# A last batch's routing moved among attention tiles, a square root behind one scatter, another output bank, and earlier norms, in a gated cross-attention and mixture-of-experts block

## The chip, the cores and the metric

The kernel runs on one core of one Trainium2 chip. The metric is the device time of one execution in microseconds; lower is better.

## The reference

Sixteen batches of 112 tokens with 512 channels pass through a gated cross-attention and then a gated mixture of experts. Everything is fp32.

```
x = x + tanh(g_xattn) * xattn(layernorm(x), ctx)      # ctx: 16 x 375 x 128, 16 heads, rotated queries and keys
x = x + tanh(g_ffn)   * ffn(layernorm(x))
ffn: logits = x @ gate_w.T                            # 64 experts
     topv, topi = top_k(logits, 8); rw = softmax(topv)
     out = sum over the 8 chosen e of rw_e * down_e(silu(gate_e(x)) * up_e(x))
     out = out + sigmoid(x @ sh_gate1.T) * shared_expert(x)
```

## The kernel before

**Stages.** The attention goes through four groups g = 0 to 3 of four batches. A group has a head loop (h = 0 to 17) and then an attention loop (t = 0 to 62). In the head loop TensorE does for each head a projection (12 matmuls of 448 columns, `project`), the latent product (9 matmuls, `latent`), and, two heads behind, the product with the folded key weights (`to_context`); VectorE multiplies by cosines and sines (seven operations for a head, the rotation, in `latent`), and GpSimd adds the two parts. In the attention loop each step t takes one tile of 128 rows of scores: `score_tile`, a softmax over four engines, `turn_tile` (transposes, four steps later) and `attend` (once in four tiles). `out_head` then projects a batch's 16 heads to the 512 output channels; batches 12, 13 and 14 have theirs at step HALF = 49 of the last group, batch 15 (`LAST`) from step 57 on, two heads at 57, two at 59, twelve behind the loop.

**Routing of one batch.** It is cut into steps which every engine issues at the same place of its own written-out order (`finish(step, b)`): *stats* (VectorE takes mean and variance, GpSimd the power -1/2 in `spread`), *norm* (VectorE; SyncE then stores the rows and the base), *turn* (4 transposes on TensorE, a copy on ScalarE), *router* (8 short matmuls), *choose* (VectorE: top 8, mask, weights; 2.4 us), *rank* (two pairs of matmuls that count earlier tokens of each expert), *place* (VectorE: the row number of each of the 8 copies), *scatter 0* to *7* (GpSimd: eight indirect DMAs that put the token's row into the expert's slots in DRAM, `slot_rows`). VectorE counts its results of a batch in `s_route`, 16 for each; the wait of a step for 15 or 16 of a batch is a wait for *place*. Batches are strictly in order, since *rank* uses the running `count`.

**Where the steps stand.** Batches 0 to 11 are routed one group later in the head loop by `slots` and `between` (slots 2h and 2h + 1), or, the last ones of a group, beside the output heads (`held`, `beside`). A group's first routed batch has stats in slot 0, norm in slot 2 and turn in slot 3; slot 2 comes, on VectorE, behind the rotation of head 0. Batch 12 is routed in steps HALF + 1 to HALF + 11 of the last attention loop (`LATE`). Batches 13 and 14 are `held(NG)`: turn, router and rank stand beside batch 15's heads 4, 5, 9 (batch 13) and 7, 10, 15 (batch 14). Behind them GpSimd issues batch 13's eight scatters, the power for batch 15, and batch 14's eight scatters. `END` then routes batch 15 and orders the experts by load (*order*), with its own eight scatters last.

**Banks.** Batch 15's output stands in PSUM bank 7, which batch 12's routing also uses, so head 0 waits for batch 12's *place* (L993). Banks 0 to 2 hold scores.

**Experts.** `load_expert` reads an expert's weights (768 KB), `load_slots` its token rows (up to 612 KB) once all scatters have landed (`wait_attention_over`). For each expert TensorE transposes the rows (`turn`), multiplies by gate and up (`inner`) and by the down weights (`down`); VectorE and ScalarE split each operand in a high and a low part. SyncE issues expert 0's weights when the order is known, then slots 0, weights 1, slots 1, weights 2, slots 2 to 4. The results are scattered to `parts`, from which the last stage sums.

```python
                if p == NG and h == 0:
                    pe.wait_ge(s_exp, RT * B)
                    pe.wait_ge(s_route, NR * (B - GB + 1))
...
            sp.wait_ge(s_order, 1)
            load_expert(0)
            wait_attention_over(sp)
            for x in range(NXE):
                load_slots(sp, x)
                if 1 <= x + 1 < NE:
                    load_expert(x + 1)
```

Of the kernel before, what the change touches and what calls it, by code (L numbers as in the profile page):

```python
# [29 lines left out]
GB = 4  # L30
# [81 lines left out]
NR = 16  # L112
# [23 lines left out]
def slots(g, i):  # L136

    at = START[LEFT[g]][i]
    whole = {"turn": at + 3, "router": at + 4, "choose": at + 5, "rank": at + 7, "place": at + 8}
# [19 lines left out]
def held(p):  # L159

    if p == NG:
        return [B - 3, B - 2]
# [11 lines left out]
LATE_LOADED = 16 * 13  # L174
FIRST_LATE = B - GB
LATE = {HALF + 1: ("norm", FIRST_LATE), HALF + 2: ("turn", FIRST_LATE), HALF + 3: ("norm", FIRST_LATE + 1),
        HALF + 4: ("router", FIRST_LATE), HALF + 5: ("choose", FIRST_LATE), HALF + 6: ("norm", FIRST_LATE + 2),
        HALF + 7: ("rank", FIRST_LATE), HALF + 8: ("place", FIRST_LATE), HALF + 9: ("scatter low", FIRST_LATE),
        HALF + 11: ("scatter high", FIRST_LATE)}

# [26 lines left out]
def route_banks(b):  # L207
# [5 lines left out]
    if b in held(NG):  # L213
        return 0, 1 + b % 2, 3
# [5 lines left out]
def out_bank(b):  # L220
    return OUT_BANK[b % GB] if b < B - GB else 4 + b % GB
# [61 lines left out]
def build(nc, a, out):  # L283
    with ExitStack() as ctx:
# [252 lines left out]
        def sync(sp):  # L537
# [166 lines left out]
            for g in range(NG):  # L704
# [40 lines left out]
                for t in range(GB * RT + ALL_LAGS):  # L745
# [5 lines left out]
                    if g == NG - 1 and LATE.get(t):  # L751
                        finish(*LATE.get(t))
# [66 lines left out]
        def tensor(pe):  # L819
# [157 lines left out]
            def out_head(p, h, part):  # L977
# [82 lines left out]
            for g in range(NG):  # L1060
# [21 lines left out]
                for t in range(GB * RT + ALL_LAGS):  # L1082
# [5 lines left out]
                    if g == NG - 1 and LATE.get(t):  # L1088
                        finish(*LATE.get(t))
# [60 lines left out]
            for x in range(E + 1):  # L1150
# [4 lines left out]
                if x >= 1:  # L1155
                    down(x - 1)
# [57 lines left out]
        def vector(dve):  # L1214
# [217 lines left out]
            for g in range(NG):  # L1432
# [24 lines left out]
                for t in range(GB * RT + ALL_LAGS):  # L1457
# [10 lines left out]
                    if g == NG - 1 and LATE.get(t):  # L1468
                        finish(*LATE.get(t))
# [93 lines left out]
            turn(0)  # L1563
            find_own(0)
# [6 lines left out]
            for x in range(E + 1):  # L1571
# [518 lines left out]
```

## Time and profile before

| | |
|---|---|
| median of 3 runs | 1543.54 us (1543.45 to 1543.58) |
| the profiled execution | 1545.0 us, its span 1543.1 us |
| TensorE busy | 1419.2 us (92%) |
| VectorE, GpSimd, ScalarE busy | 1147.3, 783.3, 672.1 us |
| mean granted TensorE clock | 0.970 of full speed |
| DMA | 380.10 MB, mean 246 GB/s |

The span runs from the first to the last instruction on the profiled core. The program's four attention groups take its first two thirds (to about 1070 us), the experts run from about 1104 to 1451 us, and the rest is the final sum.

### The profile page before, as it was taken

What the parts mean: (1) busy time and instruction counts of PE and PEld (TensorE: products, weight loads), DVE (VectorE), ACT (ScalarE), POOL (GpSimd) and SP (SyncE); (2) the same over time, 40 slices, a digit from 0 to 9 for tenths busy, and PEclk for the clock granted to TensorE, in tenths of its full rate; (3) what the DMA queues carried; (4) which work ended last, traced back from release to release, by engine and by line L of the source; (5) the groups of instructions that cost most, each with busy time, mean ns of one, the idle gap of its engine ahead of it and who ended that gap; (6) DMA issues with size and microseconds to landing.
All of it is one profiled execution on the core that took longest, in us unless ns stands there. A gap on an engine that the chain in (4) does not pass through costs nothing.

```text
span 1543.1 us, 25067 instructions
## 1 busy us (share of the span) xinstructions
PE 1419.2 (92%) x7674; PEld 1165.1 (76%) x7674; DVE 1147.3 (74%) x2601; ACT 672.1 (44%) x1558; POOL 783.3 (51%) x858
## 2 busy tenths in 40 slices
PE   6999899899999989999989999986399999989985
PEld 5767787777788777778877778864388999979742
DVE  5777783298987269989528988544488999979587
ACT  3332673011476011177301137431277777867521
POOL 4555673145775458877345786325344344334322
PEclk9999999999999999999999999998599999999998
DMA  7898896355697757830365763295899999999698
GB/s 238 298 313 314 274 286 193 112 167 188 215 307 219 265 162 246 253 122 8 104 217 191 243 216 113 86 341 180 239 331 327 332 357 366 373 339 338 206 429 344
DMA packets 164359, 380.10 MB, mean 246 GB/s; under 512 B 20200, under 2 KB 55682, under 8 KB 162434
## 3 DMA queue, kind: packets, MB, share of 16 engines
q1 hardware_dynamic: 136182, 286.33, 55.5%
q0 software_dynamic: 20608, 62.28, 11.8%
q10 hardware_dynamic: 7436, 29.88, 6.0%
q8 instruction: 64, 1.05, 0.3%
q14 instruction: 69, 0.57, 0.1%
HBM read 238.82 MB, written 139.59 MB: 245 GB/s over the span
## 4 chain that ended last, share of the span: by engine, by line
PE 71%; DVE 10%; DMA 9%; issue 5%; POOL 2%; ACT 2%; SPq 1%; POOLq 0%; another core or an unknown queue 0%; DVEq 0%; ACTq 0%
PE bank L822 18%; PE bank L824 17%; PE bank L823 17%; PE bank L926 8%; PE bank L955 4%; DMA p_in<-parts 3%; PE bank L1124 2%; DMA parts<-y_sb,to_row 1%; DMA w_ex<-in_w_ex 1%; PE bank L914 1%; PE bank L904 1%; DMA out<-p_sum 1%; DVE prob_t0l L1309 1%; POOL slot_rows L1962 1%; ACT prob L1705 1%
## 5 line engine op out<-in xcount | busy, mean ns | idle before, releaser
L1940 POOL TENSOR_TENSOR q_rope<-q_rope,q_sin 128x448 f32<-128x448 f32 x192 | 215.7, 1153 | 147.4 <-DVE q_sin L1274 146.8
L2020 POOL DMA_INDIRECT parts<-y_sb,to_row x140 | 138.3, 988 | 221.0 <-ACT y_sb L1846 191.4
L1946 POOL TENSOR_TENSOR prob<-prob,row_inv 128x375 f32<-128x375 f32 x219 | 176.8, 814 | 88.7 <-DVE row_inv L1296 86.5
L1962 POOL DMA_INDIRECT slot_rows<-rows,pos_i x112 | 109.7, 980 | 104.2 <-DVE count L1384 76.8
L1274 DVE TENSOR_TENSOR q_sin<-bank,sin_q 128x448 f32<-128x448 f32 (+1 forms) x256 | 158.5, 619 | 4.0
L926 PE MATMUL bank<-q_rope,m_w 128*128 128x448 f32 x384 | 155.7, 541 | 2.8 <-issue 1.8
L1288 DVE TENSOR_REDUCE row_max<-bank 128x1 f32<-128x375 f32 x224 | 118.9, 535 | 36.8 <-PE bank L824 36.4
L1705 ACT ACTIVATE prob<-bank,row_max 128x375 f32<-128x375 f32 x224 | 128.3, 573 | 9.1 <-DVE row_max L1288 9.1
L1846 ACT ACTIVATE y_sb<-bank,own 96x512 f32<-96x512 f32 (+4 forms) x140 | 90.9, 687 | 68.6 <-PE bank L824 62.0
L955 PE MATMUL bank<-ident,prob 128*125 128x128 f32 x672 | 113.6, 279 | 7.1 <-DVE prob_t0l L1309 3.6
L1270 DVE TENSOR_TENSOR q_rope<-bank,cos_q 128x448 f32<-128x448 f32 x192 | 118.3, 616 | 0.0
L955 PEld LDWEIGHTS bank<-ident,prob 128*125 128x125 f32 x672 | 103.6, 189 | 15.9 <-POOL prob L1946 13.1
L926 PEld LDWEIGHTS bank<-q_rope,m_w 128*128 128x128 f32 x384 | 71.5, 189 | 53.4 <-issue 50.3
L1688 ACT ACTIVATE q_th<-bank 128x448 fp32r<-128x448 f32 x64 | 34.9, 545 | 170.6 <-PE bank L926 156.4
L1681 ACT ACTIVATE q_hk0h<-bank 128x448 fp32r<-128x448 f32 x32 | 17.5, 546 | 160.4 <-PE bank L824 160.4
L1720 ACT ACTIVATE prob_t0h<-bank 125x384 fp32r<-125x384 f32 x128 | 63.0, 492 | 46.0 <-PE bank L955 46.0
L1124 PE MATMUL bank<-ident,x_g 96*128 96x96 f32 (+4 forms) x560 | 64.5, 261 | 20.0 <-DMA x_g<-slot_rows 20.0
L1124 PEld LDWEIGHTS bank<-ident,x_g 96*128 96x128 f32 (+4 forms) x560 | 59.5, 144 | 29.6 <-DMA x_g<-slot_rows 20.5
L822 PE MATMUL bank<-xg_t0h,w_gu_s0h 128*128 128x224 f32 (+5 forms) x256 | 75.9, 297 | 4.9 <-DVE e_half L1529 4.9
L1342 DVE SCALAR_TENSOR_TENSOR x_sb<-bank,tanh_g,x_sb 112x512 f32<-112x512 f32 x16 | 11.3, 746 | 88.5 <-PE bank L824 88.5
L822 PE MATMUL bank<-xg_t1h,w_gu_s1h 128*128 128x224 f32 (+5 forms) x256 | 73.9, 289 | 0.7 <-DVE e_half L1529 0.6
L823 PE MATMUL bank<-xg_t0l,w_gu_s0h 128*128 128x224 f32 (+5 forms) x256 | 73.2, 286 | 0.0
(364 smaller groups left out, 4399.1 us busy)
## 6 DMA issues: line engine op xcount, KB each, us to landing
w_ex<-in_w_ex SPq DMA_DIRECT2D x64, 768.0 KB
slot_rows<-blank SPq DMA_DIRECT2D x64, 612.0 KB
p_in<-parts SPq DMA_DIRECT2D x14, 2048.0 KB, 16.9
m_w<-m_dram SPq DMA_DIRECT2D x48, 192.0 KB
x_g<-slot_rows ACTq DMA_DIRECT2D x16, 476.0 KB
wq_s0h<-wq_dram SPq DMA_DIRECT2D x24, 256.0 KB
wq_s0l<-wq_dram SPq DMA_DIRECT2D x24, 256.0 KB
wq_s1h<-wq_dram SPq DMA_DIRECT2D x24, 256.0 KB
```

What stands on the lines that cost most here:

```text
L822: pe.matmul(out_ap, wh, mh, start=first, stop=False)
L823: pe.matmul(out_ap, wh, ml, start=False, stop=False)
L824: return pe.matmul(out_ap, wl, mh, start=False, stop=last)
L926: m = pe.matmul(bank[5][:, 0:GT], m_w[n % NW][:, c, :], q_rope[h % 2][:, c, :], start=(c == 0), stop=(c == QC - 1))
L955: m = pe.transpose(bank[bk][0:LP, j * P:(j + 1) * P], prob[n % NP][:, j * LP:(j + 1) * LP], ident[:])
L1124: m = pe.transpose(bank[n % 3][:, j * size:(j + 1) * size], x_g[x % NXE][0:size, t, j * P:(j + 1) * P], ident[0:size, 0:size])
L1274: dve.tensor_tensor(q_sin[to:to + size, other, :].rearrange("p (b s) -> p b s", b=GB), src[at:at + size], table, ALU.mult).then_inc(s_rope, 1)
L1705: act.activation(prob[i][:], bank[score_bank(n)][:, 0:L], ACT.Exp, bias=row_max[:, i:i + 1], accum_out=row_sum[:, i:i + 1]).then_inc(s_exp, 1)
L1940: pool.tensor_tensor(o[:, c, :], o[:, c, :], q_sin[:, c, :], ALU.add).then_inc(s_radd, 1)
L1946: pool.tensor_tensor(prob[i][:], prob[i][:], row_inv[:, i:i + 1].to_broadcast([P, L]), ALU.mult)\
L1962: pool.indirect_dma_start(slot_rows, bass.IndirectOffsetOnAxis(ap=pos_i[i][:, k:k + 1], axis=0), rows[i][:], None).then_inc(s_slots[i], 16)
L2020: pool.indirect_dma_start(parts, bass.IndirectOffsetOnAxis(ap=to_row[x % NROW][0:size, t:t + 1], axis=0), y_sb[x % NY][t][0:size, :], None)\
```

## The change

It has five parts. (1) The first routed batch of a group has its norm in slot 1 and its turn in slot 2, so the norm is issued on VectorE ahead of head 0's rotation. (2) Batch 13's turn, router, choose, rank, place and all eight scatters stand in steps HALF + 9 to HALF + 12 of the last attention loop; only batch 14 is held, at heads 4, 5 and 9. (3) Batch 15's output stands in bank 2; head 0 waits no longer for batch 12's place, and batch 13's turn waits until batch 12's ranks have been read from bank 7. (4) GpSimd takes batch 15's power behind scatter 0 of batch 14. (5) The weights of experts 0 to 2 are all issued when the order is known; expert 0's `inner` is issued before expert 1's `turn`, on VectorE and ScalarE too, with both splits of weights ahead; slots 5 are loaded behind `inner(0)` as before.

```diff
-    whole = {"turn": at + 3, "router": at + 4, ...
+    whole = {"turn": at + (3 if i else 2), "router": at + 4, ...
-    return {"stats": max(0, at - 2), "norm": max(2, at), **(whole if i < GB - LEFT[g] else {})}
+    return {"stats": max(0, at - 2), "norm": at if i else 1, **(whole if i < GB - LEFT[g] else {})}
...
-        return [B - 3, B - 2]
+        return [B - 2]
...
-          NG: ({"turn": 4, "router": 5, "rank": 9}, {"turn": 7, "router": 10, "rank": 15})}.get(
+          NG: ({"turn": 4, "router": 5, "rank": 9},)}.get(
...
+STATS_AT = 1
-        HALF + 7: ("rank", FIRST_LATE), HALF + 8: ("place", FIRST_LATE), HALF + 9: ("scatter low", FIRST_LATE),
-        HALF + 11: ("scatter high", FIRST_LATE)}
+        HALF + 7: [("rank", FIRST_LATE)], HALF + 8: [("place", FIRST_LATE)],
+        HALF + 9: [("scatter low", FIRST_LATE), ("turn", FIRST_LATE + 1)], HALF + 10: [("router", FIRST_LATE + 1)],
+        HALF + 11: [("scatter high", FIRST_LATE), ("choose", FIRST_LATE + 1)],
+        HALF + 12: [("rank", FIRST_LATE + 1), ("place", FIRST_LATE + 1), ("scatter low", FIRST_LATE + 1),
+                    ("scatter high", FIRST_LATE + 1)]}
...
-        return 0, 1 + b % 2, 3
+        return 0, 1, 3
...
 def out_bank(b):
+    if b == LAST:
+        return 2
...
-                    pe.wait_ge(s_route, NR * (B - GB + 1))
...
+                    elif b == B - GB + 1:
+                        pe.wait_ge(s_route, NR * (b - 1) + R_RANKED)
...
-            load_expert(0)
+            for x in range(NE):
+                load_expert(x)
             wait_attention_over(sp)
             for x in range(NXE):
                 load_slots(sp, x)
-                if 1 <= x + 1 < NE:
-                    load_expert(x + 1)
...
             turn(0)
-            for x in range(E + 1):
+            inner(0)
+            turn(1)
+            for x in range(1, E + 1):
...
-                    if b == LAST - 1:
-                        finish("stats", LAST)
-                    finish("scatter low", b)
-                    finish("scatter high", b)
+                    for k in range(TOP):
+                        if b == LAST - 1 and k == STATS_AT:
+                            finish("stats", LAST)
+                        finish(f"scatter {k}", b)
```

## Rows read from the trace of the kernel before

**Rows 1.** The page: the chain that ended last, share by engine

```profile
PE 71%; DVE 10%; DMA 9%; issue 5%; POOL 2%; ACT 2%; SPq 1%; POOLq 0%; another core or an unknown queue 0%; DVEq 0%; ACTq 0%
```

**Rows 2.** Windows: stretch, then busy us per engine, granted clock, DMA share, GB/s

```profile
1064.00:1110.00 46.00, 12.90 (x61) 10.21 (x60) 17.92 (x69) 4.38 (x10) 23.98 (x26) 0.58 0.70 216
1300.00:1400.00 100.00, 95.18 (x731) 87.48 (x729) 89.71 (x213) 74.35 (x135) 36.91 (x39) 0.97 1.01 351
```

**Rows 3.** Timeline, TensorE at the starts of groups 1, 2, 3: start, duration, instruction, idle before

```profile
303.65 1.01 PE L1028 MATMUL bank<-ident,early_rows 112*128 112x112 f32 x4 [4.17 <-DVE early_rows L1399]
...
308.10 0.37 PE L822 MATMUL bank<-q_hk1h,wcq_s1h 128*128 128x448 f32 x1
...
548.19 0.37 PE L822 MATMUL bank<-q_hk0h,wcq_s0h 128*128 128x448 f32 x1
...
549.82 0.36 PE L824 MATMUL bank<-q_hk0h,wcq_s0l 128*128 128x448 f32 x1
554.35 1.01 PE L1028 MATMUL bank<-ident,rows 112*128 112x112 f32 x4 [4.17 <-DVE rows L1399]
...
559.65 0.36 PE L822 MATMUL bank<-q_hk1h,wcq_s1h 128*128 128x448 f32 x1
...
806.42 1.01 PE L1028 MATMUL bank<-ident,rows 112*128 112x112 f32 x4 [4.17 <-DVE rows L1399]
```

**Rows 4.** Timeline, GpSimd and VectorE at the start of group 2

```profile
548.38 0.57 POOL L1906 TENSOR_TENSOR ln_stats<-ln_stats,minus_half 112x1 f32<-112x1 f32 x1
...
549.50 0.61 DVE L1270 TENSOR_TENSOR q_rope<-bank,cos_q 128x448 f32<-128x448 f32 x1
...
553.58 0.71 DVE L1399 TENSOR_SCALAR rows<-x_sb,ln_stats 112x512 f32<-112x512 f32 x1
```

**Rows 5.** Timeline, the last attention steps and batch 15's heads

```profile
1040.91 0.24 ACT L1705 ACTIVATION_READ_ACCUMULATOR prob<-bank,row_max 128x1 f32 x1
...
1043.98 0.55 DVE L1309 TENSOR_TENSOR prob_t0l<-bank,prob_t0h 125x384 fp32r<-125x384 f32 x1
...
1044.32 0.74 PE L822 MATMUL bank<-v_w0h,q_th 128*112 128x512 f32 x1 [3.23 <-DVE count L1384]
...
1047.92 0.48 PE L822 MATMUL bank<-prob_t0h,kv_r1h 125*128 125x512 f32 x1
...
1068.03 0.40 PE L824 MATMUL bank<-v_w2h,q_tl 128*112 128x512 f32 x1
```

**Rows 6.** Timeline, VectorE on batch 15: residual, norm, slot numbers

```profile
1069.64 0.74 DVE L1342 SCALAR_TENSOR_TENSOR x_sb<-bank,tanh_g,x_sb 112x512 f32<-112x512 f32 x1
...
1075.69 0.55 DVE L1399 TENSOR_SCALAR rows<-x_sb,ln_stats 112x512 f32<-112x512 f32 x1 [4.36 <-POOL ln_stats L1904]
...
1083.78 0.17 DVE L1383 CAST pos_i<-place 112x8 int32<-112x8 f32 x1
```

**Rows 7.** Timeline, GpSimd: first scatter of batch 12 and of batch 13

```profile
1044.23 1.06 POOL L1962 DMA_INDIRECT slot_rows<-rows,pos_i  x1 [1.76 <-DVE count L1384]
...
1064.53 0.94 POOL L1962 DMA_INDIRECT slot_rows<-rows,pos_i  x1 [10.51 <-DVE count L1384]
```

**Rows 8.** Timeline, SyncE's issues and TensorE at the experts' start

```profile
1089.99 0.01 SPq L774 DMA_DIRECT2D w_ex<-in_w_ex  x1
1099.21 0.34 SPq L533 DMA_DIRECT2D x_g<-slot_rows  x1
...
1103.91 2.18 PE L1124 MATMUL bank<-ident,x_g 96*128 96x96 f32 x12 [16.61 <-DMA x_g<-slot_rows]
...
1111.37 0.59 PE L822 MATMUL bank<-xg_t0h,w_gu_s0h 128*128 128x288 f32 x1
...
1117.64 0.38 PE L822 MATMUL bank<-xg_t1h,w_gu_s1h 128*128 128x288 f32 x1
```

**Rows 9.** The chain in order of time: start, us, what

```profile
1094.57 3.19 DMA slot_rows<-rows,pos_i
...
1361.91 16.17 DMA w_ex<-in_w_ex
```

More of the change, by code:

```diff
@@ L138, in slots @@
     at = START[LEFT[g]][i]
-    whole = {"turn": at + 3, "router": at + 4, "choose": at + 5, "rank": at + 7, "place": at + 8}
+    whole = {"turn": at + (3 if i else 2), "router": at + 4, "choose": at + 5, "rank": at + 7, "place": at + 8}
     if g:
         whole.update({f"scatter {k}": at + 9 + (k * 7 // 8 if i == 2 else k) for k in range(TOP)})
-    return {"stats": max(0, at - 2), "norm": max(2, at), **(whole if i < GB - LEFT[g] else {})}
+    return {"stats": max(0, at - 2), "norm": at if i else 1, **(whole if i < GB - LEFT[g] else {})}
 def between(g, slot):
@@ L174 @@
 LATE_LOADED = 16 * 13
+STATS_AT = 1
 FIRST_LATE = B - GB
[L176 to L179 removed]
+LATE = {HALF + 1: [("norm", FIRST_LATE)], HALF + 2: [("turn", FIRST_LATE)], HALF + 3: [("norm", FIRST_LATE + 1)],
+        HALF + 4: [("router", FIRST_LATE)], HALF + 5: [("choose", FIRST_LATE)], HALF + 6: [("norm", FIRST_LATE + 2)],
+        HALF + 7: [("rank", FIRST_LATE)], HALF + 8: [("place", FIRST_LATE)],
[3 more added lines that the diff above has]
+                    ("scatter high", FIRST_LATE + 1)]}
 LAST = B - 1
@@ L750, in sync @@
                         load_early()
-                    if g == NG - 1 and LATE.get(t):
-                        finish(*LATE.get(t))
+                    for step, b in LATE.get(t, ()) if g == NG - 1 else ():
+                        finish(step, b)
                     if t < GB * RT:
@@ L1087, in tensor @@
                             out_head(NG - 1, h, "all")
-                    if g == NG - 1 and LATE.get(t):
-                        finish(*LATE.get(t))
+                    for step, b in LATE.get(t, ()) if g == NG - 1 else ():
+                        finish(step, b)
                     if 0 <= t - TURN_LAG < GB * RT:
@@ L1154, in tensor @@
                     inner(x)
-                if x >= 1:
-                    down(x - 1)
+                down(x - 1)
             def body(eng, r, x):
@@ L1467, in vector @@
                         project_out(NG - 1)
-                    if g == NG - 1 and LATE.get(t):
-                        finish(*LATE.get(t))
+                    for step, b in LATE.get(t, ()) if g == NG - 1 else ():
+                        finish(step, b)
                     if attend_at(t - 1):
@@ L1562, in vector @@
             split_expert(0)
-            turn(0)
-            find_own(0)
+            split_expert(1)
             dve.tensor_scalar(l_room, bank[7][0:1, E:2 * E], float(-TR), 0.0, ALU.add, ALU.max).then_inc(s_rounds, 1)
@@ L1570, in vector @@
             dve.tensor_tensor(starts[:], l_at, l_first, ALU.add).then_inc(s_rounds, 1)
-            for x in range(E + 1):
+            turn(0)
+            inner(0)
+            find_own(0)
+            turn(1)
+            find_own(1)
+            for x in range(1, E + 1):
                 if x + 1 < E:
@@ L1783, in scalar @@
                             finish("choose", b)
-                    if g == NG - 1 and LATE.get(t):
-                        finish(*LATE.get(t))
+                    for step, b in LATE.get(t, ()) if g == NG - 1 else ():
+                        finish(step, b)
                     if attend_at(t - 1):
@@ L1849, in scalar @@
             split_expert(0)
+            split_expert(1)
             turn(0)
-            for x in range(E + 1):
+            inner(0)
+            load_slots(act, NXE)
+            turn(1)
+            for x in range(1, E + 1):
                 if x + 1 < E:
@@ L1996, in gpsimd @@
                         project_out(NG - 1)
-                    if g == NG - 1 and LATE.get(t):
-                        finish(*LATE.get(t))
+                    for step, b in LATE.get(t, ()) if g == NG - 1 else ():
+                        finish(step, b)
                     if EARLY_SCORES <= t - 2 < GB * RT:
```

3 lines of the change are left out of this document (1 added, 2 removed).

## The prediction

> **What bounds the kernel now.** I read first the chain that ended last [rows 1]: 71% of it is TensorE, 10% VectorE, 9% DMA. TensorE is busy 92% of the span, so a change can gain only where it is left waiting, and what a wait is worth must be read at its place. I then went through the stretches in windows, and the low ones are two kinds. One is the stretch in which batch 15 is finished and the experts start, 1064 to 1110: TensorE is busy 12.9 of 46.0 us at a granted clock of 0.58, and GpSimd, with 24.0 us, is the busiest engine [rows 2]. The other is short: in the timelines of TensorE at the starts of groups 1, 2 and 3 there is the same hole of 4.17 us each time, in front of the four transposes (L1028) of the group's first routed batch, ended by VectorE's norm [rows 3]. The experts' stretch is different: from 1300 to 1400 TensorE is busy 95.2 of 100 us, VectorE 89.7, and the DMA share is 1.01 [rows 2]. There nothing is gained by order alone, but a later start or an earlier one is passed on to the end.
>
> **Part 1, the groups' first norm.** Group 2 shows why the hole is there [rows 3, 4]. TensorE issues its last matmul of head 0's latent product at 549.82 and would turn the routed batch next. GpSimd has that batch's power ready at 548.38 + 0.57 = 548.95. But VectorE begins the rotation at 549.50, and its norm stands behind it and begins at 553.58; the transposes start at 554.35. With the norm ahead, VectorE takes it at about 549.1 (0.15 behind the power, an estimate for the hand-over) and ends by 549.8, when TensorE comes. So the hole goes: 3 x 4.17 = 12.5 us.
>
> What it costs: VectorE waits some 1.1 us for GpSimd's power ahead of head 1's projection split, and the norm holds that split and the rotation up by about 0.6 us. Behind them queue GpSimd's additions and, a head later, `to_context`. The cover is TensorE's own work between: 12 matmuls of projection and 9 of the next latent product, 21 x 0.204 = 4.3 us (0.204 is the step from 548.19 to 549.82 over eight [rows 3]). The rotation takes 553.58 - 549.50 = 4.1 us, so it ends at about 554.2, GpSimd's last addition at about 555.8, and `to_context` of head 0 starts behind turn, projection, latent product and router at about 555.4 and asks for the last third a little after 556.5. It holds, with under 1 us to spare; if that cover were gone, each group would give back up to 0.6 us. SyncE stores rows and base one slot earlier, two issues of some 0.34 us each (as another load's [rows 8]), ahead of loads needed over 4 us later: nothing.
>
> The hole has a second price. Behind it the granted clock is at its lower level, 1.2 of 2.4 GHz: in group 2 turn and projection take 559.65 - 554.35 = 5.30 us. At the full level 12 x 448 + 4 x 112 columns at 0.204 us for 448 are 2.7 us. That is 2.6 us, in group 1 (308.10 - 303.65 = 4.45) 1.75 us, and for group 3 I take group 2's [rows 3]. Without a hole TensorE runs straight on, as it did up to 549.82. Sum 7.0 us; the bounds are 0 and 7.0 (a little work might still be slow), and I take 7.0, since the four transposes are then all that interrupts dense matmuls.
>
> Part 1: 19.5 us.
>
> **Parts 2 to 4, up to the last scatter.** Head 0 of batch 15 started at 1044.32 after 3.23 us for batch 12's place. What it still needs is the last exponential, 1040.91 + 0.24 = 1041.15 [rows 5]. So heads 0 and 1 start at 1041.3, 3.0 us earlier. Into the next two steps come batch 13's turn, its copy on ScalarE and its router. VectorE's low part of tile 53, which the transposes of tile 55 need, is still behind batch 12's place and ends at 1044.53 [rows 5]. `attend` of block 2 started at 1047.92; it can't start before about 1045.0 now, nor later than 1047.9 unless the copy stalls. I take 1046.2, since turn, copy and router are a round trip of some 2 us, part of it under other transposes. From there to the end of batch 15's heads were 1068.43 - 1047.92 = 20.5 us; batch 13's turn and router (about 1 us, from the 1.01 us of four transposes at the low clock [rows 3] and eight shorter matmuls) have left it: 19.5. The heads end at 1065.7 (1064.5 to 1067.4).
>
> GpSimd now. From 1064.53 to 1094.57 it starts 24 scatters and one power, so one each (30.04 - 1.15) / 23 = 1.25 us [rows 7, 9]. Batch 12's eight run from 1044.23 to 1054.2 as before. Batch 13's place needs rank, behind `attend` (9 matmuls) and heads 2 and 3: about 1050, and 2.4 us on VectorE: 1052.5, before GpSimd is free. So batch 13's scatters, which started at 1064.53, are done at 1064.2. Scatter 0 of batch 14 ends at 1065.5. Batch 14's turn, router and rank stand where batch 13's stood, 3 us earlier, so its place is ready by then.
>
> Residual and statistics of batch 15 took from 1069.64 to 1075.69 - 4.36 = 1071.33, 1.7 us; VectorE comes to them only when batch 14's place is done, 1.2 us late. Now it is free: 0.1 + 1.7, then addition and power, 1.1 with hand-overs (the power 0.57 [rows 4]). The norm starts 2.9 us behind the last head: 1068.6 against 1075.69 [rows 6]. GpSimd stands idle for 2 us in front of that power, which is harmless only as far as the following queue isn't the later end: fifteen scatters follow, the last starts at 1068.7 + 14 x 1.25 = 1086.2. Batch 15's place ends 8.3 us behind its norm (1083.95 - 1075.69 [rows 6]), 1076.9, and its first scatter is due at 1077.5, so GpSimd stays the bound, narrowly. Last scatter 1094.57 to 1086.2: 8.4 us.
>
> **Part 5.** The first weights were issued 14.3 us behind the norm (1089.99); now at 1082.9, and three of them, 2.36 MB. At 351 GB/s [rows 2] that is 6.7 us alone, but the scatters (112 rows of 2176 bytes in 1.25 us, 195 GB/s) run until 1087. I get 1092.5 for the third weight. The first slots' load was issued 4.6 us behind the last scatter's start, landed 4.7 us later [rows 8, 9], and is now issued at 1090.8, so it can stand behind weights for 1.6 us, or, if the scatters come first, up to 1.57 MB / 351 = 4.5 us; below nothing is excluded, since it was alone before. I take 1.0. The rows arrive at 1103.91 - 8.4 + 1.0 = 1096.5: 7.4 us gained (3.9 to 9.5).
>
> The Trainium skill (DMA: Bandwidth & Descriptors, Queues, rings and completion order) says that each DMA engine takes turns between its queues packet by packet. By that the scatters' packets would wait beside the weights' and the last one would land later than its 3.19 us; if it shared evenly, its 244 KB would take twice as long, about 0.7 us more by 351 GB/s. No row before shows scatters beside three weights.
>
> From the first rows' arrival to expert 1's `inner` were 1117.64 - 1103.91 = 13.7 us [rows 8]. Now: transposes and splits 3.4, `inner(0)` 5.5 (1111.37 on, low clock), `turn(1)` 1.6, its splits on ScalarE and VectorE 2 to 2.5, of which `turn(2)` hides its own time only: 13.0. That is 0.7 us (0 to 2), since the wait for expert 1's splits takes the place of the one for its rows.
>
> **Sum.** 12.5 + 7.0 + 7.4 + 0.7 = 27.6 us, off a span of 1543.1: 1515.5. The profiled execution took 1545.0, the median of the runs is 1543.54, 0.4 above that span: 1515.9.
>
> **Rivals.**
> 1. *The weights hold up the slots.* For it: one queue, in order, and 1.57 MB more ahead of the slots. Against: they are issued 8 us before. It costs up to 4.5 instead of 1.0: 1519.4. Chance 0.13.
> 2. *The experts catch up.* The chain has a weight load of 16.17 us at 1361.91 [rows 9], the only big wait in the experts' stretch, and TensorE lost 4.8 of 100 us there [rows 2]. With two weights out of the opening rush the DMA is 4.5 us ahead: up to that much more gained, 1511.4. Against: a load waits for its buffer, so a lead is not kept. Chance 0.12.
> 3. *The groups' wait returns one step later.* TensorE would wait for the copy, the delayed rotation or a weight load, each time, and keep part of the hole. If it keeps half of hole and clock, 9.7 us: 1525.6. For it: under 1 us to spare. Against: VectorE idles after the old norm. Chance 0.08.
> 4. *The DMA makes it slower.* The share is 1.01 from 1300 to 1400 [rows 2]. If the new order of loads made each of the 64 experts wait longer for weights, the gain is gone from 27.6 / 64 = 0.43 us an expert on; at 0.5 us it is 32.0: 1547.9. Against: the bytes are the same and SyncE's order from expert 3 on is too. Chance 0.02.
> 5. *Nothing moves*: parts 1 to 4 each take away a wait that TensorE or GpSimd shows in its own timeline, so 0.01.
>
> The forecast itself, 1512.5 to 1519, has 0.64. About 0.2% (3.1 us) is what a measurement can tell from no change. Faster 0.96, same 0.01, slower 0.03. Down to rival 2 and up beyond rival 1: 1510.5 to 1521.5.
>
> **What would show it.** In the timeline of TensorE no idle time in front of L1028 in groups 1 to 3, and 0.204 us steps behind it; VectorE's norm ahead of the first rotation. Head 0 at about 1041.3 - 19.5 = 1021.8; batch 13's scatters without a pause behind batch 12's; the norm of batch 15 at 1049, the last scatter's start at 1066.7, the first rows at 1077, all on the new time axis. The forecast is wrong if GpSimd's queue has a pause before batch 14's scatter 1 longer than 4 us, if the first slots take over 7 us to land, or if the experts' stretch, 347 us from 1104 to 1451, is not 346 to 347.

## The result, and the profile after

The changed kernel takes 1523.55 us (median of 4 runs, 1520.89 to 1530.97), the kernel before 1543.56 us in the same rounds (1543.45 to 1544.13): a ratio of 0.9877, 95% interval 0.9843 to 0.9912, so 20.0 us faster. The forecast was 1515.9 us with a range of 1510.5 to 1521.5. The direction is right; the gain is 7.6 us smaller than forecast, and the time lies above the range. The profiled execution took 1523.96 us for a span of 1522.1.

The chain that ended last (compare [rows 1]) is still TensorE's, with two points less of it and two more of GpSimd:

```profile
PE 69%; DMA 10%; DVE 10%; issue 5%; POOL 4%; ACT 2%; SPq 0%; POOLq 0%; ACTq 0%; DVEq 0%
```

Lines after have other numbers: L827 to L829 are the three products of a split matmul, L1034 the turn, L1046 the router, L1406 the norm, L1920 the power, L1976 the scatter, L1130 the transposes of an expert's rows. At the start of group 2 TensorE's timeline has no hole in front of the turn (it was 4.17 us, [rows 3]):

```profile
542.38 0.36 PE L827 MATMUL bank<-q_hk0h,wcq_s0h 128*128 128x448 f32 x1
...
542.79 0.37 PE L829 MATMUL bank<-q_hk0h,wcq_s0l 128*128 128x448 f32 x1
543.00 0.55 PE L1034 MATMUL bank<-ident,rows 112*128 112x112 f32 x4
...
543.81 0.36 PE L829 MATMUL bank<-xn_th,wq_s0l 128*128 128x448 f32 x1
544.01 0.36 PE L827 MATMUL bank<-xn_th,wq_s0h 128*128 128x448 f32 x1
```

The four transposes take 0.55 us instead of 1.01, the steps behind them are 0.2 us, and the granted clock is 1.00 there (0.50 behind the hole before). From the turn to the next latent product (`q_hk1h`) it takes 2.88, 2.84 and 2.83 us in groups 1, 2 and 3, where it took 4.45, 5.30 and 5.32, and none of the three has a hole. Late attention on TensorE, with batch 13's turn and router among the heads (compare [rows 5]):

```profile
1021.02 0.56 PE L960 MATMUL bank<-ident,prob 128*125 128x128 f32 x3 [1.08 <-DVE prob_t0l L1316]
1021.75 0.46 PE L827 MATMUL bank<-v_w0h,q_th 128*112 128x512 f32 x1 [0.16 <-DVE q_tl L1322]
...
1023.21 0.55 PE L1034 MATMUL bank<-ident,rows 112*128 112x112 f32 x4
...
1040.49 0.39 PE L829 MATMUL bank<-v_w2h,q_tl 128*112 128x512 f32 x1
```

VectorE's norm of batch 15 and GpSimd's first and last scatter of the last four batches (compare [rows 6, 7]):

```profile
1046.78 0.55 DVE L1406 TENSOR_SCALAR rows<-x_sb,ln_stats 112x512 f32<-112x512 f32 x1 [4.17 <-POOL ln_stats L1920]
```

```profile
1024.72 1.06 POOL L1976 DMA_INDIRECT slot_rows<-rows,pos_i  x1 [1.76 <-DVE count L1391]
1026.09 0.94 POOL L1976 DMA_INDIRECT slot_rows<-rows,pos_i  x1 [0.30 <-issue]
...
1064.39 0.94 POOL L1976 DMA_INDIRECT slot_rows<-rows,pos_i  x1 [0.30 <-issue]
```

The pause of 10.51 us in front of batch 13's first scatter [rows 7] is gone, 32 scatters (those of batches 12 to 15) run on end with one power among them, and the last one starts 30.2 us earlier than the 1094.57 of before. From there the lead shrinks. The chain in order of time (compare [rows 9]) has this scatter's landing at 8.66 us, where it was 3.19:

```profile
1064.39 8.66 DMA slot_rows<-rows,pos_i
1073.97 4.71 DMA x_g<-slot_rows
```

What the DMA moved in that landing, by queue (packets, MB, share of the 16 engines; q0 carries GpSimd's scatters, q1 SyncE's loads), before (1094.57 to 1097.76) and after (1064.39 to 1073.05):

```profile
q0 software_dynamic: 264, 0.77, 69.6%
q1 hardware_dynamic: 2, 0.01, 0.5%
```

```profile
q1 hardware_dynamic: 296, 1.60, 46.7%
q0 software_dynamic: 359, 1.05, 30.1%
```

The scatters alone are more than the last one's 244 KB: earlier ones are still on their way when it is issued. After, 1.60 MB of weights move beside them.

And the experts' start, in the timelines of SyncE, TensorE and ScalarE (compare [rows 8]; the last four are the load of slots 5 that ScalarE issues, ScalarE's split of expert 1's rows, the next expert's transposes, and expert 1's first product):

```profile
1059.72 3.37 SPq L780 DMA_DIRECT2D w_ex<-in_w_ex  x3
...
1073.97 5.07 SPq L539 DMA_DIRECT2D x_g<-slot_rows  x5
...
1078.72 2.18 PE L1130 MATMUL bank<-ident,x_g 96*128 96x96 f32 x12 [20.32 <-DMA x_g<-slot_rows]
...
1089.79 0.40 ACTq L539 DMA_DIRECT2D x_g<-slot_rows  x1
1090.23 1.25 ACT L1831 ACTIVATE xg_t1h<-bank 128x384 fp32r<-128x384 f32 x3 [4.40 <-DVE to_row L1566]
1091.46 2.15 PE L1130 MATMUL bank<-ident,x_g 96*128 96x96 f32 x12 [2.48 <-DVE xg_t1l L1520]
...
1093.32 0.59 PE L827 MATMUL bank<-xg_t1h,w_gu_s1h 128*128 128x288 f32 x1
```

The slots' load takes 4.8 us from issue to the transposes, as before. Expert 1's first product is 14.6 us behind the first rows, where it was 13.7, and ScalarE had stood idle for 4.40 us just before.

The windows from expert 1's first product to the last store of parts, before and after:

```profile
1117.64:1453.82 336.18, 329.81 (x2472) 300.32 (x2471) 301.52 (x699) 256.25 (x463) 137.34 (x140) 0.99 0.97 331
```

```profile
1093.32:1432.43 339.11, 332.28 (x2471) 301.90 (x2470) 301.13 (x697) 256.11 (x462) 136.23 (x139) 0.99 0.94 322
```

The stretch is 2.9 us longer. In its middle, from 1300 to 1400, TensorE is as busy as in [rows 2], and the DMA share is the same:

```profile
1300.00:1400.00 100.00, 95.22 (x734) 87.04 (x733) 90.04 (x213) 74.22 (x135) 37.42 (x38) 0.98 1.01 350
```

Laid end to end, the lead on the span is: 19.5 us at the last transposes in front of batch 15's head 0 (1040.53 to 1021.02), 30.2 at the last scatter, 25.2 at the first rows (1103.91 to 1078.72), 24.3 at expert 1's first product, 21.4 at the last store (1453.82 to 1432.43), 21.0 at the end (1543.1 to 1522.1). The forecast had 27.9, 26.9, 27.6 and 27.6 for the last scatter, the rows, expert 1 and the end.

### The profile page after: what moved, and what is told of

It is laid out like the page before. It is cut to its first block, busy times and chain, and to the rows that moved or that the text cites. A ratio compares the mean times of both kernels' runs of the same rounds, so it can differ in the third digit from the quotient of the medians.

```text
span 1522.1 us, 25067 instructions
## 1 busy us (share of the span) xinstructions
PE 1412.8 (93%) x7674; PEld 1160.2 (76%) x7674; DVE 1149.3 (76%) x2601; ACT 672.2 (44%) x1558; POOL 782.4 (51%) x858
## 3 DMA queue, kind: packets, MB, share of 16 engines
q8 instruction: 64, 1.05, 0.3%
## 4 chain that ended last, share of the span: by engine, by line
PE 69%; DMA 10%; DVE 10%; issue 5%; POOL 4%; ACT 2%; SPq 0%; POOLq 0%; ACTq 0%; DVEq 0%
PE bank L827 18%; PE bank L829 17%; PE bank L828 17%; PE bank L931 8%; PE bank L960 4%; DMA p_in<-parts 3%; PE bank L1130 2%; DMA parts<-y_sb,to_row 2%; DMA w_ex<-in_w_ex 2%; POOL slot_rows L1976 2%; PE bank L919 1%; POOL q_rope L1954 1%; PE bank L909 1%; DMA out<-p_sum 1%; ACT prob L1716 1%
## 5 line engine op out<-in xcount | busy, mean ns | idle before, releaser
L1976 POOL DMA_INDIRECT slot_rows<-rows,pos_i x112 | 109.6, 979 | 94.0 <-DVE count L1391 66.0
L1130 PE MATMUL bank<-ident,x_g 96*128 96x96 f32 (+4 forms) x560 | 64.5, 261 | 22.8 <-DMA x_g<-slot_rows 20.3
L1130 PEld LDWEIGHTS bank<-ident,x_g 96*128 96x128 f32 (+4 forms) x560 | 59.5, 144 | 32.3 <-DMA x_g<-slot_rows 20.5
L827 PE MATMUL bank<-xg_t0h,w_gu_s0h 128*128 128x224 f32 (+5 forms) x256 | 75.8, 296 | 6.6 <-DVE e_half L1536 5.3
L827 PE MATMUL bank<-xg_t1h,w_gu_s1h 128*128 128x224 f32 (+5 forms) x256 | 74.8, 292 | 0.8 <-DVE e_half L1536 0.7
```

Of the source, the lines that this page charges most:

```text
L827: pe.matmul(out_ap, wh, mh, start=first, stop=False)
L1130: m = pe.transpose(bank[n % 3][:, j * size:(j + 1) * size], x_g[x % NXE][0:size, t, j * P:(j + 1) * P], ident[0:size, 0:size])
L1976: pool.indirect_dma_start(slot_rows, bass.IndirectOffsetOnAxis(ap=pos_i[i][:, k:k + 1], axis=0), rows[i][:], None).then_inc(s_slots[i], 16)
```

## The experiments

The questions: what lengthened the scatter's landing and the stretch behind it, the weights or the new order of the start? And is the rest of the gain really from part 1? "Tail" below is the time from the last scatter's start to the last store in the profile. The kernel before was timed again beside each set; medians are compared by the ratio, since its own was 1545.04 (e1 to e4), 1548.45 (e5 to e8) and 1546.22 us (e9 to e11) in the three sets.

**e1, the weights at their old place.** The changed kernel with

```diff
-            for x in range(NE):
-                load_expert(x)
+            load_expert(0)
 ...
                 load_slots(sp, x)
+                if 1 <= x + 1 < NE:
+                    load_expert(x + 1)
```

> The changed kernel with SyncE's loads in the order of before: weights 0, then behind the scatters slots 0, weights 1, slots 1, weights 2, slots 2 to 4. Theory A (the three weights in flight hold up the last scatter, 8.66 us to landing against 3.19): the landing is 3 to 4 us again, the first slots are issued some 5 us earlier than in the changed kernel. Slots 1 come later beside weights 1, but inner(0) covers them: 3 to 5 us faster than the changed kernel, about 1519. Theory B (the denser scatters themselves make the landing slow): the landing stays near 8.7 us and the time within 1 us of the changed kernel, 1523.5.

1537.10 us (1534.48 to 1538.74), 0.9942 (0.9927 to 0.9958). The landing is 3.70 us again, so the early weights are what lengthened it (theory A). But the kernel is slower, not faster: its tail is 367.9 us, as long as the changed kernel's 368.0, because rows to expert 1 now take 19.7 us instead of 14.6. The chain in order of time says why:

```profile
1083.12 7.16 DMA w_ex<-in_w_ex
1090.31 1.06 ACT w_gu_s1h L1840
1091.40 1.23 DVE w_gu_s1l L1527
...
1093.97 1.41 DVE xg_t0l L1521 x3
...
1102.93 0.27 DVE found L1559
...
1103.42 0.40 ACTq L539
...
1103.87 0.50 ACT xg_t1h L1832
1104.39 0.57 DVE xg_t1l L1521
```

In the new order VectorE splits expert 1's weights ahead of expert 0's rows, so `inner(0)` waits for weights that it does not use; behind it `find_own(0)` (`found`), ScalarE's load and expert 1's splits follow one after the other. The new start order needs the early weights, and the 1519 us that theory A gave are missed by 18 us for this reason.

**e2, the experts' start order of before**, weights early:

```diff
-            inner(0)
-            turn(1)
-            for x in range(1, E + 1):
+            for x in range(E + 1):
 ...
-                down(x - 1)
+                if x >= 1:
+                    down(x - 1)
```

and likewise on VectorE (`turn(0)`, `find_own(0)`, then the loop) and ScalarE, each as in the kernel before.

> The changed kernel with expert 1's turn ahead of expert 0's inner on TensorE, VectorE and ScalarE, and the splits as before; the three weights stay early. Theory A (ScalarE's copies of expert 1's rows wait behind the load of slots 5, which waits for find_own(0) behind inner(0), so TensorE idles 2.5 us and its clock falls): expert 1's inner starts at most 13 us behind the first rows instead of 14.9, with no wait at turn(2): 2 to 4 us faster than the changed kernel, about 1520.5. Theory B (the start order is not what costs; the experts' stretch is set by the DMA): no difference beyond 1 us.

1530.78 us (1525.37 to 1532.13), 0.9904 (0.9886 to 0.9922). The tail falls to 358.9 us, 9.1 less than after, with a landing still of 6.95 us: rows to expert 1 take 10.2 us instead of 14.6, and the stretch behind 336.3 instead of 339.1. Yet the time does not follow, since the last scatter started at 1075.33, not 1064.39. Something before it was late, and this profile shows what: VectorE at batch 14's choosing. The idle time before it is put down to "remote": a semaphore that it waits for was updated just before it began, but no instruction of the kernel that updates it had ended in the 1.5 us before. GpSimd's row is the wait for that batch's place.

```profile
1046.40 0.23 DVE L1357 MAX8 top<-bank 112x8 f32<-112x64 f32 x1 [11.81 <-remote]
1050.88 0.94 POOL L1968 DMA_INDIRECT slot_rows<-rows,pos_i  x1 [7.18 <-DVE count L1390]
```

**e3, part 1 alone**: the kernel before with only the new `turn` and `norm` entries of `slots`.

```diff
-    whole = {"turn": at + 3, ...
+    whole = {"turn": at + (3 if i else 2), ...
-    return {"stats": max(0, at - 2), "norm": max(2, at), ...
+    return {"stats": max(0, at - 2), "norm": at if i else 1, ...
```

> The kernel before with part 1 alone: norm in slot 1, turn in slot 2. By the prediction's step 19.5 us off: 1524.0, and the changed kernel's other four parts are then worth together only about 0.5 us in the time. Rival: part of the 19.5 us was not in it and the late parts gave the rest: 1528 to 1533.

1525.37 us (1524.51 to 1527.41), 0.9869 (0.985 to 0.9887): 19.7 us faster than the 1545.04 beside it, against 19.5 forecast for this part. It is as fast as the whole change, as far as the intervals can tell.

**e4, parts 1 to 4**: e2 with the load order of before as well, so that nothing of part 5 is left.

> The changed kernel without part 5: loads and start order both as before, parts 1 to 4 kept. Theory A (part 5 costs in both of its halves, the last scatter is started 10.7 us earlier by parts 2 to 4 and 19.5 by part 1): the whole stretch behind the last scatter is as before, so 1543.5 - 30.2 = 1513.3. Theory B (the DMA sets the experts' stretch, so an earlier start is partly lost there): 1517 to 1522.

1524.99 us (1521.87 to 1527.61), 0.9860 (0.9839 to 0.9881). That is neither of its theories (1513.3, and 1517 to 1522), and against e3 nothing that the intervals can tell. The tail is the shortest, 357.9 us, but the last scatter started at 1076.92, even later than e3's 1072.73, behind the same standstill:

```profile
1037.76 0.38 ACT L1734 ACTIVATE q_th<-bank 128x256 fp32r<-128x256 f32 x1 [7.35 <-remote]
```

```profile
1047.68 0.23 DVE L1358 MAX8 top<-bank 112x8 f32<-112x64 f32 x1 [9.08 <-remote]
```

**e5, the changed kernel again, unchanged, in a later set of executions.** Does the standstill belong to the variants or to single executions?

> The changed kernel once more, beside the next three, since its own profile shows batch 15's heads without a pause while the profiles of e1, e2 and e4, whose code up to there is the same, show ScalarE idle 4 to 6 us and then VectorE 6 to 11 us in the middle of batch 14's routing with nothing they wait for done late. Theory S (a stall from outside the program's own waits that falls in some executions): this one shows it now, the last scatter starts near 1076 instead of 1064.4, and the time is 1525 to 1532. Rival (the stall belongs to the other kernels' programs): no stall, 1523.5 again.

1532.45 us (1526.92 to 1538.08), 0.9903 (0.9876 to 0.9931). It shows it. The same instruction in the first profile of the changed kernel, then in this one:

```profile
1032.85 0.23 DVE L1358 MAX8 top<-bank 112x8 f32<-112x64 f32 x1 [0.78 <-PE bank L1046]
```

```profile
1043.79 0.94 POOL L1976 DMA_INDIRECT slot_rows<-rows,pos_i  x1 [0.30 <-issue]
...
1046.16 0.23 DVE L1358 MAX8 top<-bank 112x8 f32<-112x64 f32 x1 [11.90 <-remote]
...
1050.65 0.94 POOL L1976 DMA_INDIRECT slot_rows<-rows,pos_i  x1 [5.92 <-DVE count L1391]
```

The last scatter starts at 1075.93 here and at 1064.39 there, 11.5 us apart, with identical code. So what parts 2 to 4 bring depends on the execution. The record doesn't tell on which chip the first set ran, so that a difference of chips isn't excluded for this pair; but on each of two chips there is a profile with over 9 us at this MAX8 and one, of the same code up to there, with under 4 (e5 and e8, e9 and e11).

**e6 and e7, batch 13's scatters held back.** If the standstill comes from scatters on end, a gap should remove it. e4 (as e6) and e2 (as e7) with batch 13's eight scatters out of the attention tiles, waiting for batch 14's slot numbers, and batch 15's power behind the fourth of them:

```diff
-        HALF + 12: [("rank", FIRST_LATE + 1), ("place", FIRST_LATE + 1), ("scatter low", FIRST_LATE + 1),
-                    ("scatter high", FIRST_LATE + 1)]}
+        HALF + 12: [("rank", FIRST_LATE + 1), ("place", FIRST_LATE + 1)]}
 ...
+                    if b == LAST - 2:
+                        pool.wait_ge(s_route, NR * (LAST - 1) + R_POS)
```

> e4 with batch 13's eight scatters held on GpSimd until batch 14's slots are known, so that only eight scatters run beside the end of batch 15's heads, and batch 15's power behind the fourth of them. In e4, e1 and e2 VectorE comes back from its stall just when the scatters' stream ends (1047.7, 1048.2, 1046.4). Theory S1 (the engines' own instruction loads wait behind the stream of scatters): the stall shrinks to under 3 us, the last scatter starts near 1069 in place of 1076.9, and the time is about 7 us under e4's, 1518. Theory S2 (the stall is bound to a place in the code): it is as long as before; 24 scatters then start at about 1050, the last at 1080, and it is 3 us slower than e4, 1528.

> e2 (three weights early, start order of before) with the same hold on batch 13's scatters. By theory S1 1516 to 1520, the fastest of all, as e2's experts' stretch (346.4 us from the first rows to the last scatter of results) is the shortest; by S2 about 1533. If early weights are worth nothing it equals e6.

e6: 1530.86 us (1526.59 to 1531.4), 0.9881 (0.9857 to 0.9904). e7: 1527.28 us (1524.74 to 1532.44), 0.9867 (0.9844 to 0.9890). VectorE's wait at the MAX8 falls from 9.08 and 11.81 us to 1.88 and 3.75 us. ScalarE's hardly does, 7.35 and 5.86 us to 6.14 and 5.25. The times are above what theory S1 gave (1518, and 1516 to 1520). In e6 the last scatter still starts at 1075.90, for now GpSimd itself stands idle:

```profile
1045.06 0.94 POOL L1968 DMA_INDIRECT slot_rows<-rows,pos_i  x1 [11.54 <-DVE count L1390]
```

One standstill was exchanged for another; no gain.

**e8, the new start order mended.** In the changed kernel ScalarE's load of slots 5 needs `find_own(0)`, which stands behind `inner(0)` on VectorE, and expert 1's splits stand behind that load on ScalarE. Here `find_own(0)` goes ahead of `inner(0)`, and the load behind `turn(1)`:

```diff
 # VectorE
             turn(0)
-            inner(0)
             find_own(0)
+            inner(0)
 # ScalarE
             inner(0)
-            load_slots(act, NXE)
             turn(1)
+            load_slots(act, NXE)
```

> The changed kernel with find_own(0) ahead of inner(0) on VectorE and the load of slots 5 behind turn(1) on ScalarE. Theory A (ScalarE's copies of expert 1's rows waited behind that load and find_own(0), and the idle TensorE lost its clock): expert 1's inner starts at most 13 us behind the first rows, in place of 14.6, TensorE has no wait over 1 us there, and the stretch from the last scatter to the last result scatter is 363 us or less in place of 368; 4 to 7 us faster than e5. Rival (inner(0) ahead of turn(1) costs by itself, since expert 1's splits are then bare): 13.5 us or more, at most 2 us faster than e5.

1530.74 us (1521.96 to 1537.12), 0.9897 (0.9872 to 0.9922); the profiled span, 1520.1 us, is the shortest of all. ScalarE's row after (4.40 us behind `to_row`) has become

```profile
1090.36 1.25 ACT L1831 ACTIVATE xg_t1h<-bank 128x384 fp32r<-128x384 f32 x3 [2.46 <-PE bank L1130]
```

Rows to expert 1 take 12.4 us (14.6 after, 13.0 in e5), the tail 360.6. So this wait was real and worth up to 2.2 us of that stretch. The old order with weights early (e2) still does it in 10.2. In time the difference can't be told from e5's: 1.7 us, where 4 to 7 were expected.

**e9, e10, e11, VectorE's instructions moved along.** e2 with 128 (e9) or 64 (e10) and e4 with 128 (e11) memsets of one element at the very start of VectorE's work:

```diff
+            for n in range(128):
+                dve.memset(scratch_e[0:1, n // E, n % E:n % E + 1], 0.0)
             dve.wait_ge(s_first, 32)
```

> The kernel of e2 (the changed kernel with the experts' start order of before), with 128 memsets of one element each added at the very start of VectorE's work, where it waits for the first loads (until some 9 us): nothing else differs, but every later instruction of VectorE stands 128 places further on in its stream. In e2's profile VectorE stood still 11.81 us at the MAX8 of batch 14's choosing with nothing of the program in its way, and the last scatter began at 1075.33 instead of 1064.39. Theory P (the stall belongs to a place in VectorE's instruction stream, a wait for its next instructions): the MAX8 of batch 14 waits under 2 us, the last scatter begins at 1064 to 1068, the time falls by 5 to 10 us against e2 (1519 to 1526 on a chip where before takes 1545), and a stall of some us may stand about 128 instructions earlier instead. Theory Q (it belongs to that instruction, its operands or the moment in the kernel): still 9 to 12 us at that MAX8, last scatter near 1075, the ratio of e2 (0.990).

> As e9 with 64 memsets instead of 128. Theory P: again under 2 us at the MAX8 of batch 14; if a stall stands elsewhere, it stands 64 instructions later than in e9. Theory Q: 9 to 12 us at that MAX8, ratio about 0.990.

> The kernel of e4 (parts 1 to 4 alone; load order and start order of the experts as before) with the same 128 memsets at the start of VectorE's work. e4's profile had 9.08 us of standstill at that MAX8 and its last scatter at 1076.92. Theory P: under 2 us there, last scatter at 1065 to 1069, span about 8 us shorter than e4's 1524.5, ratio 0.981 to 0.983. Theory Q: as e4, ratio 0.986.

e9: 1527.22 us (1525.54 to 1531.16), 0.9877 (0.9845 to 0.9909). e10: 1531.18 us (1519.62 to 1533.06), 0.9883 (0.9831 to 0.9934). e11: 1526.55 us (1522.97 to 1530.87), 0.9886 (0.9851 to 0.9921). In e9 and e10 the standstill is where it was, 11.26 and 10.53 us at the same MAX8:

```profile
1039.72 0.75 PE L827 MATMUL bank<-v_late5h,q_th 128*112 128x512 f32 x1
...
1047.49 0.23 DVE L1357 MAX8 top<-bank 112x8 f32<-112x64 f32 x1 [11.26 <-remote]
```

TensorE had gone on to the next head at 1039.72, so the router's product that MAX8 waits for was done some 7 us before it began. Its signal was not. In e11 it is gone (1.87 us), but 3.75 us of the same kind stand at batch 13's rank:

```profile
1034.58 0.23 DVE L1383 TENSOR_TENSOR rank_sb<-bank,expert_entries 112x64 f32<-112x64 f32 x1 [3.75 <-remote]
```

The same 128 left it in place in e9, so e11 is no proof of a place in the stream. Theory P falls for these two shifts.

**What the engines wait for.** The trace also records when each semaphore is updated. MAX8 waits for TensorE's signal that the router's last product is done. In after, that update stands 0.01 us behind the product's end. In the six profiles in which MAX8 idles over 9 us it stands 6.0 to 8.8 us behind the end, and MAX8 begins 0.02 to 0.03 us after it:

| | product's end | TensorE's signal | MAX8 begins |
|---|---|---|---|
| after | 1032.81 | 1032.82 | 1032.85 |
| e1 | 1042.13 | 1048.18 | 1048.20 |
| e2 | 1037.61 | 1046.38 | 1046.40 |
| e4 | 1041.62 | 1047.66 | 1047.68 |
| e5 | 1038.67 | 1046.14 | 1046.16 |
| e9 | 1039.96 | 1047.46 | 1047.49 |
| e10 | 1040.06 | 1047.55 | 1047.57 |

ScalarE's wait is of the same kind: the signal for its `q_th` comes 2.1 to 5.6 us behind the product's end in e1 to e11, and 0.01 in before and after. The ends of matmuls are modelled in the profile, but late products can't be the whole of it: in e9 the signals of four heads, whose products end from 1041.32 to 1045.07, stand at 1047.52, 1047.57, 1047.62 and 1047.67. So VectorE and ScalarE didn't stand still by themselves; TensorE's signals reached them late and in a bunch.

The trace speaks against theory S1, as far as it shows instruction loads: the DMA queues of that kind have no packet between 1017 and 1048 in e2 and e4, and none from 1041 to 1048 in e5 and e9, so none ends near the end of the wait. What stays is a coincidence in time. The windows of e9 around it (columns as in [rows 2]; the last two are the DMA share and GB/s):

```profile
1044.00:1045.00 1.00, 1.00 (x3) 0.30 (x1) 0.00 (x0) 0.00 (x0) 0.34 (x1) 0.58 0.56 183
1045.00:1046.00 1.00, 0.07 (x1) 0.00 (x0) 0.00 (x0) 0.00 (x0) 0.00 (x0) 1.00 0.64 198
1046.00:1047.00 1.00, 0.00 (x0) 0.00 (x0) 0.00 (x0) 0.00 (x0) 0.00 (x0) 1.00 0.07 28
1047.00:1048.00 1.00, 0.00 (x0) 0.00 (x0) 0.48 (x4) 0.00 (x0) 0.00 (x0) 1.00 0.00 0
```

and of e2:

```profile
1045.00:1046.00 1.00, 0.00 (x0) 0.00 (x0) 0.00 (x0) 0.00 (x0) 0.00 (x0) 0.50 0.19 65
1046.00:1047.00 1.00, 0.00 (x0) 0.00 (x0) 0.57 (x5) 0.00 (x0) 0.00 (x0) 0.50 0.00 0
```

VectorE resumes within about 1.5 us of the end of the scatters' transfers: 1046.40 in e2, 1047.49 in e9; in e5 1046.16, the transfers' share falling from 0.70 to 0.18 in that microsecond.

The marks of all profiles in one table (us; "landing" is from the last scatter's start to the issue of the first slots' load, "load" from there to the first rows' transposes; the MAX8 is batch 14's, but batch 13's in before and e3, where that batch stands at the same heads):

| | MAX8 idle | last scatter | landing | load | rows to expert 1 | expert 1 to last store | tail | span |
|---|---|---|---|---|---|---|---|---|
| before | 2.30 | 1094.57 | 4.6 | 4.7 | 13.7 | 336.2 | 359.2 | 1543.1 |
| after | 0.78 | 1064.39 | 9.6 | 4.8 | 14.6 | 339.1 | 368.0 | 1522.1 |
| e5, the same | 11.90 | 1075.93 | 8.5 | 4.9 | 13.0 | 337.7 | 364.2 | 1530.2 |
| e1 | 9.10 | 1077.39 | 4.6 | 5.2 | 19.7 | 338.3 | 367.9 | 1535.2 |
| e2 | 11.81 | 1075.33 | 7.9 | 4.6 | 10.2 | 336.3 | 358.9 | 1523.5 |
| e3 | 1.13 | 1072.73 | 5.1 | 4.5 | 14.1 | 337.5 | 361.2 | 1523.6 |
| e4 | 9.08 | 1076.92 | 4.4 | 4.6 | 13.3 | 335.5 | 357.9 | 1524.5 |
| e6 | 1.88 | 1075.90 | 3.9 | 4.9 | 16.1 | 338.9 | 363.8 | 1529.2 |
| e7 | 3.75 | 1078.83 | 4.6 | 4.8 | 10.7 | 339.7 | 359.8 | 1527.9 |
| e8 | 3.56 | 1069.80 | 6.4 | 4.6 | 12.4 | 337.2 | 360.6 | 1520.1 |
| e9 | 11.26 | 1078.08 | 9.1 | 5.2 | 9.8 | 337.6 | 361.7 | 1529.2 |
| e10 | 10.53 | 1077.99 | 9.2 | 4.6 | 10.4 | 338.7 | 362.9 | 1530.6 |
| e11 | 1.87 | 1070.11 | 5.7 | 4.4 | 13.8 | 337.1 | 361.0 | 1520.9 |

## Why the prediction missed, step by step

In the sum, part 1 was 19.5 us and parts 2 to 5 together 8.1 (8.4 - 1.0 + 0.7). Measured are 19.7 for part 1 alone (e3) and 20.0 for everything, so it is the 8.1 us that did not come.

**Part 1 was right in mechanism and size.** Forecast 12.5 us of holes and 7.0 of clock, 19.5. In the profile after the holes are gone, and the stretches behind them are 1.6, 2.5 and 2.5 us shorter, 6.5 together. Its lead at the first mark is 19.51; that it agrees to the last digit is luck, for in e3's profile the same mark is 20.4 us earlier. The time of e3 is 19.7 us lower, good to some 3 us. Rival 3 (the wait returns one step later) did not come.

**Parts 2 to 4 were right in mechanism in one profile.** In the profile after the last scatter gained 30.2 - 19.5 = 10.7 us, where 8.4 was forecast. Two sizes were off. Head 0 started at 1021.75 (forecast 1021.8), but the heads ended 1065.7 - 19.5 = 1046.2 by forecast and 1040.9 in fact: I had carried over 19.5 us of the old timeline, with its matmuls at the low clock (head 0's first 0.74 us [rows 5], 0.46 after). And the norm began 5.9 us behind the last head's end instead of 2.9, since the power stands behind batch 13's scatters and one of batch 14's. That cost nothing: GpSimd's queue was the bound, as forecast, from batch 12's first scatter to the last. In the other profiles with these parts the gain isn't there: against the 1072.73 of part 1 alone (e3) the last scatter starts earlier in three of nine (after, e8 and e11, by 8.3, 2.9 and 2.6 us) and 2.6 to 5.4 us later in the other six.

**The step that failed in the profile after is Part 5.** The prediction put it at a loss of 1.0 us for the weights and a gain of 0.7 us for the order, -0.3 together. From the last scatter's start to the last store it is -5.0 (landing 9.6 instead of 4.6), -0.1, -0.9 (14.6 instead of 13.7) and -2.9 (the experts' stretch 339.1 instead of 336.2, a term that the sum had at nothing): 8.9 us, of which 2.3 us were made good, by luck, by the larger term before. 19.5 + 10.7 - 8.9 - 0.4 at the end is 20.9, the 21.0 of the span. The last 1.0 us of the miss lies outside it: the median stands 1.4 us above the profiled span, where 0.4 was taken over. Of the prediction's own signs of being wrong only the third came: from the first rows to the last store it is 353.7 us, where it was 349.9. Two of Part 5's premises failed:

- *The weights delay the last scatter, not the slots' load behind them.* I had looked for the delay in SyncE's queue, where the slots stand behind three weights, and had taken the scatter's 3.19 us over. The slots' load took 4.8 us as before. The scatter took 8.66, 6.95, 7.63, 5.52, 8.18 and 8.30 us with early weights in flight (after, e2, e5, e8, e9, e10), and 3.70, 4.22, 3.52, 3.03 and 4.80 us with late ones (e1, e3, e4, e6, e11). In e7 the weights are early too, but had landed when the last scatter started, and it took 3.71. The Trainium skill (DMA: Bandwidth & Descriptors, Queues, rings and completion order) has the two queues take turns packet by packet. The direction agrees. The price of 0.7 us for an equal share was too low because it counted the last scatter's 244 KB alone. In after 1.05 MB of scatters moved until it had landed, and beside them 1.60 MB of weights; at 351 GB/s those weights are 4.6 us (an estimate), most of the 5.5 us by which the landing grew. An equal share would have been 1.05 MB, 3.0 us, so the weights got more than that. On its own this delay was nearly made up: with the old start order the tail is 358.9 with weights early and 357.9 with weights late.
- *The new start order costs instead of gaining 0.7 us.* With weights early it lengthens the tail by 9.1 us (after against e2), with weights late by 10.0 (e1 against e4). But single profiles of one start order differ by 4 us: e5 has 364.2, and e9 and e10, which have e2's start and loads, 361.7 and 362.9. So with early weights the cost is 1.3 to 9.1 us. I had costed TensorE's own steps, and not what ScalarE's queue holds behind `inner(0)`: the load of slots 5 and, through it, `find_own(0)` on VectorE, the chain of e1 in its plainest form. e8 shows that this wait is part of it. The rest is argued only: `inner(0)` runs with nothing to overlap it, from 1082 on (granted clock 0.50 until 1086), where the old order turned expert 1's rows first, while the first splits were still being made.

The 2.9 us in the experts' stretch are not settled: e2 and e4, with the old order, have 336.3 and 335.5, but e7, e9 and e10, with it too, have 337.6 to 339.7, so it isn't the order alone.

**What no step had: the late signals.** The forecast named a pause of GpSimd's queue of over 4 us ahead of batch 14's scatter as what would make it wrong. There was none in the first profile, and 5.92 us in the second (e5). Its cost is the 11.5 us between the two last scatters. Of nine profiles with parts 2 to 4 and their scatters on end, six show over 9 us of idle time at the MAX8 (e1, e2, e4, e5, e9, e10), and three at most 3.6 (after, e8, e11). Shown: what VectorE waits for is TensorE's signal, recorded 6.0 to 8.8 us behind the product's end. The wait goes down when batch 13's scatters are held back (e6, e7), is absent with part 1 alone (e3) and in the kernel before, varies between executions of one code, and is at neither of two shifts tied to a place in VectorE's instructions. ScalarE's smaller wait (4.0 to 7.5 us in e1 to e11, 1.9 after, 3.2 before) is one for a late signal of TensorE too; in e3 it is there without batch 13's scatters, beside batch 12's. Not shown: what holds the signals up. That they queue behind the scatters' transfers would fit the end of the wait in e2, e5 and e9, but it is argued only, and in after the same transfers ran without it. A kernel with the scatters on end but little data in each was not tried.

The times prove nothing here. The changed kernel spreads over 10 us (1520.89 to 1530.97) where before spreads over 0.7 in the same rounds, but in the later sets before spreads over 5.8, 9.8 and 9.4 us itself, and the changed kernel (e5) over 11.2.

So the 20.0 us are those of part 1. Parts 2 to 5 together measure as nothing that the intervals (some 3 to 5 us either way) can tell: 0.9877 for the whole change and 0.9903 when it was run again (e5, 16.0 us), 0.9869 for part 1 alone, 0.9860 for parts 1 to 4. Of rivals, 1 (weights in the way) had the right suspect and the wrong place; 2 (the experts catch up) did not come, the stretch got longer; 4 and 5 did not come. None of the variants is shown to be faster than part 1 alone, which also has the narrowest spread of the variants (2.9 us in four executions).

## What to carry to other kernels

Price a reordering on every engine's queue, not on the one that computes: the step which looked free here failed on a load that ScalarE had to issue and on an index that VectorE made too late. When a large transfer is moved earlier, ask which small one on another queue is now in flight beside it; the last scatter, which everything waits for, is the wrong neighbour. And before crediting an edit with a gain in one profile, take a second profile of the same code: here a wait of 12 us was in one and not in the other, while the part that simply removed a 4 us hole three times delivered its 19.5 us. Where a wait's releaser looks long done, look for the time of its signal, not only for the end of its work.

## What the runs showed of the hardware

A removed hole on TensorE gave back more than its length: 12.5 us of holes brought 19.5 to 19.7 us, since the work behind them ran at a granted clock of 1.00 instead of 0.50 to 0.62 (four transposes 0.55 us instead of 1.01).

The last of a row of scatters of 112 rows each, with 0.5 to 1.1 MB of them still to move, landed in 3.0 to 4.8 us with hardly a load beside them, and in 5.5 to 8.7 us beside 0.9 to 1.6 MB of weight loads.

With scatters on end, 1.25 us apart, TensorE's signals to VectorE and ScalarE were recorded 2.1 to 8.8 us behind the end of the products that they tell of, VectorE idled for 9 to 12 us, and it resumed about when the scatters' transfers ended. It isn't in every execution (0.01 us in the first profile of the changed kernel), and what holds the signals up is open.
